# A causal mask cut into one operation per pair of heads, in a fused attention and mixture-of-experts kernel

## The chip, the cores and the metric

The kernel runs on one core of a Trainium2 chip. The metric is device time in microseconds (us) of one execution. Engines are called PE (TensorE, matrix multiplication), DVE (VectorE), ACT (ScalarE), POOL (GpSimd) and SP (SyncE, which only issues transfers here).

## What is computed

One transformer layer on x of shape (8, 1024, 256): eight batches, 16 heads of 16 columns. Biases and the second half's expert selection are left out of this cut:

```
h = layernorm(x)
Q, K, V = h @ Wq + bq, h @ Wk + bk, h @ Wv + bv            # 16 heads of 16
logits = where(causal, Q K^T * 0.25, -inf)                  # (8, 16, 1024, 1024)
attn   = softmax(logits)
gate   = a small network of h, one number per key
x = x + ((attn * gate) @ V) @ Wo + bo
x = x + shared_expert(layernorm(x)) + two_of_eight_experts(layernorm(x))
```

The causal mask sets a probability to zero where the key comes later than the query.

## The kernel before

**Tiling.** Batch n is worked in four groups g of four heads, and each group in ten steps s. A step takes a chunk c of 512 queries and one or two tiles of 128 keys. `STEPS` lists them: for the first chunk key tile 0, then tiles 1 and 3 together, then tile 2; for the second chunk tiles 0, 1, 2, 3 and 4 one by one, then 5 and 7 together, then 6. In all but the two steps of tile 2 and tile 6 `by_pair` is true and the step's scores are made in `PAIRS` = 2 parts p, each for two heads. So a group has 8 steps of two parts and 2 steps of one part (`SCORES`). Keys of a step's tile lie along the partitions and queries along the columns.

**A step.** The item names are those of the planner, and the functions in brackets make the instructions:
- `QK` (`scores`) on PE multiplies keys by queries, once for each part p.
- `EX` (`exponent`) on ACT takes the exponential of two heads, 128x1024, into `probs`. That tile has two halves, and step s uses half s % 2. In a one-part step `EX` does all four heads at once.
- `MK` (`mask`) on POOL zeroes the triangle of a diagonal tile, 128 keys by 128 queries, in each head. Only six of a group's ten steps touch the diagonal (`DIAGONAL`): tile 0; 1 and 3; 2; 4; 5 and 7; 6. Steps with two tiles have two triangles.
- `PV` (`sums`) on PE multiplies the probabilities by the gated values. It waits for the mask where there is one, and for the last exponential where there is none. `PV` of step s frees the half of `probs` that step s + 2 writes.

**What runs beside it.** For later batches: row maxima of the scores (`M` on PE, `MR` on DVE), projections (`AQ`, `AV`) and the gate network, whose products with `ln_g`, `ln_b` and `dp_w2`, and `gt`, are POOL's. For earlier batches: the output projection, the router, the experts (`EU`, `HT`, `ED`), the scatter of tokens into slots of their experts (`SX`, line 1157, a DMA that POOL issues) and the gather and mix of results (`GY`, `CB`, `CC`, POOL too).

**The order.** Nothing but the queue's own order and semaphores decides what an engine does next. The order is made ahead by a planner, `Plan.run`: each item has an engine, a duration in its tables and a due time, and the planner takes, on the engine that can start first, the ready item that is due earliest. It also hands out the eight PSUM banks, and it prefers on PE an item of the same tiling (`FULL`, `ROWS` for `M` and `QK`, `COLS` for `PV`). Where the planner expects PE to be idle for 500 ns or more while sums are open, `keep_busy` (line 809) puts filler matmuls of 128x512 there. A changed duration or a changed list of items therefore changes the whole order behind the first place where it matters.

Of the kernel before, what the change touches and what calls it, by code (L numbers as in the profile page):

```python
# [13 lines left out]
P = 128  # L14
# [4 lines left out]
GROUP = 4  # L19
# [40 lines left out]
SCORES = [PAIRS if by_pair else 1 for _, _, by_pair in STEPS]  # L60
NSCORE = sum(SCORES)
DIAGONAL = [kts[0] >= c * QPC for c, kts, _ in STEPS]
MASKS = sum(DIAGONAL)

MAXU = [(c,) + u for c in range(CHUNKS) for u in maxima_of(c)]
NMAX = len(MAXU)
# [95 lines left out]
def step_parts(s):  # L162

    c, kts, _ = STEPS[s]
    parts, at = [], 0
    for kt in kts:
        q0 = max(c * CHUNK, kt * P)
        parts.append((kt, q0, (c + 1) * CHUNK - q0, at))
        at += (c + 1) * CHUNK - q0
    return parts  # L170
# [22 lines left out]
class Plan:  # L193
# [9 lines left out]
    def add(self, engine, item, ns, due, after=(), banks=0, tiling=None, frees=None, lands=None, spaced=None, early=0):  # L203
        self.items[item] = (engine, ns, due + LATER.get(item[0], 0), [a for a in after if a in self.items], banks, tiling, frees, lands)
        self.early[item] = early
        if spaced and spaced[0] in self.items:
            self.spaced[item] = spaced
        self.queues.setdefault(engine, {}).setdefault(item[0], []).append(item)
# [77 lines left out]
def plan_work():  # L286
    plan = Plan()
    add = plan.add

    def sums(cols, rate=0.96):  # L290
        return round(cols / rate)
# [3 lines left out]
    def step_due(n, g, s):  # L295
        return at(n, g) + GROUP_T * step_at[s] // step_at[NSTEP]
# [93 lines left out]
    def attention(n, g, s):  # L390
        c, kts, by_pair = STEPS[s]
        gs = (n * GROUPS + g) * NSTEP + s
        cols = sum(part[2] for part in step_parts(s))
        due = step_due(n, g, s)
        before = [("PV",) + divmod((gs - 2) // NSTEP, GROUPS) + ((gs - 2) % NSTEP,)] if gs > 1 else []
        for p in range(SCORES[s]):
            add("PE", ("QK", n, g, s, p), 270 + 60 * (SCORES[s] == 1 or len(kts) > 1), due + p * 1200,
                [("SM", n, g, c)] + before, 2, ROWS)
            add("ACT", ("EX", n, g, s, p), 170 + sums(2 * CHUNK, 1.2), due + p * 1200, [("QK", n, g, s, p)],
                frees=(("QK", n, g, s, p), None))  # L400
        ready = [("EX", n, g, s, p) for p in range(SCORES[s])]
        if DIAGONAL[s]:
            add("POOL", ("MK", n, g, s), 650 * len(kts), due + 1500, ready)
            ready.append(("MK", n, g, s))
        add("PE", ("PV", n, g, s), 100 * len(kts) + round(cols * 4 / 2.4), due + 4000, ready + [("VA", n, g)],
            int(s in FIRST_STEP), COLS)
        if s in LAST_STEP:
            first = ("PV", n, g, FIRST_STEP[c])
            u = (n * GROUPS + g) * CHUNKS + c
            add("ACT", ("OE", n, g, c), 490, due + 4000, [("PV", n, g, s)] + (  # L410
                [("SO", (u - 1) // (GROUPS * CHUNKS), (u - 1) // CHUNKS % GROUPS, (u - 1) % CHUNKS)] if u else []),
                frees=(first, None))
            add("SP", ("SO", n, g, c), ISSUE, due + 4000, [("OE", n, g, c)], lands=6000)
# [148 lines left out]
    for n in range(B):  # L562
        projection(n)
        gate(n)
        if n == 0:
            for i in range(FFN_CHUNKS):
                weights(i)
        for g in range(GROUPS):
            values(n, g)
            maxima(n, g)  # L570
            if g + n * GROUPS:
                pn, pg = divmod(n * GROUPS + g - 1, GROUPS)
                for s in range(NSTEP):
                    attention(pn, pg, s)
        if n:
            rest(n - 1)
    for s in range(NSTEP):
        attention(B - 1, GROUPS - 1, s)
# [4 lines left out]
def build(nc, ins, out):  # L583
    x_in = ins["x"]
    plan = plan_work()
    order, place, waits, release = plan.order, plan.place, plan.waits, plan.release
    turn_of = {item: k for k, item in enumerate(order["PE"])}
    with ExitStack() as ctx:
        def sb(name, shape, dt=F32):
            return ctx.enter_context(nc.sbuf_tensor(name, shape, dt))  # L590

        def sem(name):
            return ctx.enter_context(nc.semaphore(name))
# [68 lines left out]
        probs = sb("probs", [P, 2, GROUP, CHUNK])  # L662
# [63 lines left out]
        s_full, p_masked, pv_done = sem("s_full"), sem("p_masked"), sem("pv_done")  # L726
# [15 lines left out]
        def bank(item, j=0):  # L742
            return ps[:, place[item][j], :]
# [73 lines left out]
        block = ctx.enter_context(nc.Block())  # L817
# [194 lines left out]
        def _(pool):  # L1012
            heard = {}

            def first_wait(name, count):
# [13 lines left out]
                                    pattern=[[-1, P]], channel_multiplier=1).then_inc(const_set, 1)  # L1029
            nc.gpsimd.affine_select(out=causal, in_=causal, compare_op=ALU.is_ge, fill=NEG, base=0,  # L1030
                                    pattern=[[1, P]], channel_multiplier=-1).then_inc(const_set, 1)
            nc.gpsimd.affine_select(out=before8[:], in_=before8[:], compare_op=ALU.is_gt, fill=0.0, base=0,
                                    pattern=[[1, EXPERTS], [-1, EXPERTS]], channel_multiplier=0
                                    ).then_inc(const_set, 1)
            nc.gpsimd.affine_select(out=earlier[:], in_=earlier[:], compare_op=ALU.is_gt, fill=0.0, base=0,
                                    pattern=[[1, P]], channel_multiplier=-1).then_inc(const_set, 1)
# [80 lines left out]
                        gate[:].unsqueeze(2).to_broadcast([P, TILES, DH]), ALU.mult)  # L1117
                last.then_inc(va_built, 1)

            def mask(item, n, g, s):  # L1120
                b, k = release["EX", n, g, s, SCORES[s] - 1]
                pool.wait_ge(freed[b], k)
                for _, _, _, at in step_parts(s):
                    block = probs[:, s % 2, :, at:at + P]
                    last = nc.gpsimd.affine_select(out=block, in_=block, compare_op=ALU.is_ge, fill=0.0, base=0,  # L1125
                                                   pattern=[[0, GROUP], [1, P]], channel_multiplier=-1)
                last.then_inc(p_masked, 1)

            def normalise(item, n, q):
# [54 lines left out]
            def split_ffn(item, i):  # L1184
                if i == 0:
# [5 lines left out]

            all_work(pool, "POOL", {"PK": constants, "AR": rstd_a, "GB": gate_rstd, "GD": gate_scale, "GF": gate_dot1,
                                    "GH": gate_hidden, "GJ": gate_dot2, "VA": build_values, "MK": mask,
                                    "CP": normalise, "CK": rstd_c, "SX": scatter_tile, "GY": gather_tile,
                                    "CB": mix_one, "CC": mix_two,
# [598 lines left out]
        def _(pe):  # L1794
# [5 lines left out]
            def wait_freed(b, k):  # L1800

                if passed[b] < k:
                    pe.wait_ge(freed[b], k)
                    passed[b] = k

            def own_banks(item):
                for b, k in waits[item]:
                    wait_freed(b, k)
# [83 lines left out]
            def sums(item, n, g, s):  # L1892
                gi = n * GROUPS + g
                c = STEPS[s][0]
                first = ("PV", n, g, FIRST_STEP[c])
                if s == 0:
                    pe.wait_ge(va_built, gi + 1)
                if s in FIRST_STEP:
                    own_banks(item)
                if DIAGONAL[s]:  # L1900
                    pe.wait_ge(p_masked, gi * MASKS + sum(DIAGONAL[:s + 1]))
                else:
                    b, k = release["EX", n, g, s, SCORES[s] - 1]
                    wait_freed(b, k)
                for kt, q0, cols, at in step_parts(s):
                    for h in range(GROUP):
                        last = mm(bank(first)[32 * h:32 * h + 32, q0 - c * CHUNK:], vaug[:, kt, g, h * VW:h * VW + 32],  # L1907
                                  probs[:, s % 2, h, at:at + cols], start=(s in FIRST_STEP), stop=(s in LAST_STEP))
                last.then_inc(pv_done, 1)
# [120 lines left out]
            def expert_down(item, n, q, u):  # L2030
# [9 lines left out]
                for i in range(2):  # L2040
# [6 lines left out]
                    for j, (h, w) in enumerate(((h_hi, w2_hi), (h_hi, w2_lo), (h_lo, w2_hi))):  # L2047
# [4 lines left out]

            all_work(pe, "PE", {"AT": turn_x, "AV": values, "AQ": queries_keys, "M": maximum, "MT": turn_max,
                                "QK": scores, "PV": sums, "CW": project, "CT": turn_x2, "CG": logits, "CJ": turn_logits, "PX": place,
                                "XT": turn_slots, "EU": expert_up, "HT": turn_h, "ED": expert_down})

# [34 lines left out]
```

## Time and profile before

| | |
|---|---|
| median of 3 runs | 1828.57 us |
| lowest and highest | 1823.91 and 1830.67 us |
| span of the profiled execution | 1826.8 us, 1.8 under the median |
| other time given for the profiled execution | none, so its span stands for it |
| busy PE, DVE, ACT, POOL | 1667.4, 1297.7, 1084.0, 767.8 us |
| PE idle | 1826.8 - 1667.4 = 159.4 us |

An engine's busy time is the union of its instructions' times. PE's weight loads (PEld) lie beside its matmuls. Matmuls overlap each other's ends, so a busy PE isn't one at its peak. "Idle before" is the time an engine stood still before an instruction, and the name behind the arrow is what ended that.

### The profile page before, as it was taken

How to read it: one execution, taken by the hardware profiler on the slowest of the kernel's cores; microseconds unless marked ns; L12 is line 12 of the kernel's file. 1: busy time of each engine (PE TensorE's matmuls, PEld its weight loads, DVE VectorE, ACT ScalarE, POOL GpSimd, SP SyncE). 2: the span in 40 equal slices, each digit the busy share in tenths (PEclk: the TensorE clock that was granted, in tenths of full speed). 3: DMA queues.
4: the chain of work that ended last, by engine and by line, in shares of the span. 5: the costliest groups of instructions: out<-in, count | busy, mean ns of one | idle time of the engine just before them, and what ended most of it. 6: DMA issues, size and time to landing. Idle time of an engine off the chain costs nothing.

```text
span 1826.8 us, 34347 instructions
## 1 busy us (share of the span) xinstructions
PE 1667.4 (91%) x12734; PEld 997.3 (55%) x12734; DVE 1297.7 (71%) x2528; ACT 1084.0 (59%) x1808; POOL 767.8 (42%) x1126
## 2 busy tenths in 40 slices
PE   7798899989987999899998899999998989998798
PEld 4343356435643566456554555555664656666677
DVE  4867777967796678777686666778678657873556
ACT  2565755665556656575557756576556756568432
POOL 4424432452236211632227862353116773057760
PEclk9698999989998999999998999989999899999899
DMA  4566545554345544544434765544435674346430
GB/s 152 160 192 182 164 153 157 164 149 125 99 122 137 142 121 119 158 118 141 140 113 143 213 180 143 146 125 122 132 102 152 199 204 142 94 138 203 141 121 13
DMA packets 192707, 261.24 MB, mean 143 GB/s; under 512 B 19616, under 2 KB 127264, under 8 KB 192544
## 3 DMA queue, kind: packets, MB, share of 16 engines
q1 hardware_dynamic: 181792, 229.67, 42.9%
q0 software_dynamic: 10752, 29.37, 5.5%
q8 instruction: 105, 1.72, 0.4%
q14 instruction: 58, 0.48, 0.1%
HBM read 130.98 MB, written 127.40 MB: 141 GB/s over the span
## 4 chain that ended last, share of the span: by engine, by line
PE 44%; DMA 16%; DVE 13%; POOL 8%; ACT 7%; SPq 5%; issue 5%; DVEq 0%; POOLq 0%; ACTq 0%
PE ps_all L2017 9%; PE ps_all L1907 7%; DVE mx L1496 6%; DMA qk_s<-ql 5%; PE ps_all L2048 5%; PE ps_all L1855 5%; ACT probs L1307 4%; PE ps_all L1887 4%; PE ps_all L1839 3%; DMA xa<-in_x 3%; PE ps_all L1916 2%; PE ps_all L1825 2%; SPq L889 2%; DMA yab<-ys_s,slot_u 2%; POOL xs_s L1157 2%
## 5 line engine op out<-in xcount | busy, mean ns | idle before, releaser
L1496 DVE TENSOR_REDUCE mx<-ps_all 128x2 f32<-128x1024 f32 (+2 forms) x640 | 616.9, 1005 | 131.1 <-PE ps_all L1862 71.2
L1307 ACT ACTIVATE probs<-ps_all 128x1024 f32<-128x1024 f32 x576 | 569.2, 1027 | 185.6 <-PE ps_all L1887 182.4
L1125 POOL TENSOR_SCALAR_AFFINE_SELECT probs<-probs 128x512 f32<-128x512 f32 x256 | 160.2, 641 | 569.4 <-ACT probs L1307 567.9
L1907 PE MATMUL ps_all<-probs,vaug 128*32 128x512 f32 (+3 forms) x3072 | 323.6, 521 | 25.2 <-POOL probs L1125 22.0
L1855 PE MATMUL ps_all<-k_st,q_st 63*128 63x512 f32 (+3 forms) x1536 | 306.3, 432 | 32.5 <-DVE mx L1496 12.1
L1887 PE MATMUL ps_all<-q_st,k_st 64*128 64x512 f32 (+3 forms) x1536 | 264.2, 404 | 45.0 <-DVE mx L1496 18.5
L1855 PEld LDWEIGHTS ps_all<-k_st,q_st 63*128 63x128 f32 x1536 | 155.1, 198 | 155.4 <-issue 52.4
L1887 PEld LDWEIGHTS ps_all<-q_st,k_st 64*128 64x128 f32 x1536 | 131.3, 193 | 173.9 <-issue 67.5
L1751 DVE SCALAR_TENSOR_TENSOR act_t<-act_t,ps_all 128x256 f32<-128x256 f32 x168 | 70.4, 419 | 151.8 <-ACT act_t L1370 150.9
L2017 PE MATMUL ps_all<-w_hi,x2h 128*128 128x512 f32 (+1 forms) x480 | 167.7, 349 | 2.5 <-DVE ql L1458 1.2
L2017 PE MATMUL ps_all<-w_hi,x2l 128*128 128x512 f32 (+1 forms) x480 | 157.8, 329 | 0.0
L2017 PE MATMUL ps_all<-w_lo,x2h 128*128 128x512 f32 (+1 forms) x480 | 157.7, 329 | 0.0
L1370 ACT ACTIVATE act_t<-ps_all 128x256 f32<-128x256 f32 x168 | 64.4, 384 | 153.5 <-PE ps_all L2017 106.1
L1907 PEld LDWEIGHTS ps_all<-probs,vaug 128*32 128x32 f32 x3072 | 72.7, 111 | 140.5 <-issue 88.5
L1157 POOL DMA_INDIRECT xs_s<-xnb,slot_u x112 | 110.8, 989 | 69.8 <-issue 50.8
L1862 PE MATMUL ps_all<-bars 64*128 64x64 bf16 x2048 | 123.8, 201 | 0.0
L1169 POOL DMA_INDIRECT yab<-ys_s,slot_u x112 | 108.1, 965 | 34.0 <-issue 19.2
L2048 PE MATMUL ps_all<-w_hi,h_hi 128*128 128x256 f32 (+1 forms) x336 | 109.8, 327 | 2.0 <-DVE h_lo L1778 1.1
L2017 PEld LDWEIGHTS ps_all<-w_hi,x2h 128*128 128x128 f32 x480 | 92.2, 192 | 20.6 <-issue 11.6
L1825 PE MATMUL ps_all<-wvd,xt 128*128 128x384 f32 x256 | 98.7, 514 | 1.5 <-DMA vd_bias<-in_dp_b 0.7
L2017 PEld LDWEIGHTS ps_all<-w_hi,x2l 128*128 128x128 f32 x480 | 91.8, 191 | 8.3
L2017 PEld LDWEIGHTS ps_all<-w_lo,x2h 128*128 128x128 f32 x480 | 92.3, 192 | 5.9
(195 smaller groups left out, 2810.1 us busy)
## 6 DMA issues: line engine op xcount, KB each, us to landing
qk_s<-qh SPq DMA_DIRECT2D x116, 256.0 KB
q_st<-qk_s SPq DMA_DIRECT2D x128, 192.0 KB, 3.9
k_st<-qk_s SPq DMA_DIRECT2D x128, 192.0 KB, 4.7
xs<-xs_s SPq DMA_DIRECT2D x72, 256.0 KB
ys_s<-ysb SPq DMA_DIRECT2D x72, 256.0 KB, 3.5
o_s<-o_sb SPq DMA_DIRECT2D x64, 256.0 KB, 4.4
qk_s<-ql SPq DMA_DIRECT2D x57, 256.0 KB
xs_s<-ysb SPq DMA_DIRECT2D x20, 512.0 KB, 5.5
```

The source lines that it names most:

```text
L1125: last = nc.gpsimd.affine_select(out=block, in_=block, compare_op=ALU.is_ge, fill=0.0, base=0, pattern=[[0, GROUP], [1, P]], channel_multi ...
L1157: nc.gpsimd.indirect_dma_start(xs_s[i % 2], bass.IndirectOffsetOnAxis(ap=slot_u[:, n % 4, a, t:t + 1], axis=0), xnb[:, t, :], None).then_i ...
L1169: nc.gpsimd.indirect_dma_start(yab[:, t % 2, a, :], None, ys_s[SET_OF[n] % 2], bass.IndirectOffsetOnAxis(ap=slot_u[:, n % 4, a, t:t + 1], ...
L1307: nc.scalar.activation(to, of, ACT.Exp, scale=DH ** -0.5).then_inc(freed[release[item][0]], 1)
L1496: last = nc.vector.tensor_reduce(to[:, :, p, qt % QPC], both[:, :, at:at + keys], X_AXIS, ALU.max)
L1825: last = mm(bank(item)[:, 0:E + DP], xt[:, k, tt * P:(tt + 1) * P], wvd[:, k, :], start=(k == 0), stop=(k == KE - 1))
L1855: last = mm(bank(item, j)[:, to:to + keys], q_st[r, q_half(n, g, c), p, qt % QPC * P:(qt % QPC + 1) * P], k_st[r, k_half(n, g, kc), p, 0:k ...
L1862: last = mm(bank(item, j)[:, end:end + P // 2], bars[r, h, 1, :], bars[r, h, 0, lo:lo + P // 2], start=False, stop=(h == 1))
L1887: last = mm(bank(item, j)[:, to:to + cols], k_st[r, k_half(n, g, kt // QPC), a, kt % QPC * P:(kt % QPC + 1) * P], q_st[r, q_half(n, g, c), ...
L1907: last = mm(bank(first)[32 * h:32 * h + 32, q0 - c * CHUNK:], vaug[:, kt, g, h * VW:h * VW + 32], probs[:, s % 2, h, at:at + cols], start= ...
L2017: last = mm(bank(item)[:, to], x[:, buf, k, t * P:(t + 1) * P], w[:, k, cs], start=(k == 0 and j == 0), stop=(k == KE - 1 and j == 2))
L2048: last = mm(bank(first)[:, t * E:(t + 1) * E], h[:, z % 2, i * P:(i + 1) * P], w[:, cs], start=(item == first and i == 0 and j == 0), stop ...
```

## The change

The mask of a two-part step becomes two items, one for each part p: `MK` p waits only for `EX` p, and covers the two heads of that part. The mask of a one-part step stays one item over four heads. A group's 6 mask items become 2 x 5 = 10. Of affine selects a group had 8, each over 4 heads x 128 columns (512); it now has 12 over 2 x 128 (256) and 2 over 512. Over 32 groups that is 256 before, and 384 small and 64 of the old size now. In the planner's tables a mask item goes from 650 ns for each tile to 380 ns for each tile in a two-part step, and its due time from 1500 behind the step's to 300 for part 0 and 1500 for part 1. `PV` waits for both masks.

```
-MASKS = sum(DIAGONAL)
+MASKS = sum(n for n, d in zip(SCORES, DIAGONAL) if d)
...
         ready = [("EX", n, g, s, p) for p in range(SCORES[s])]
         if DIAGONAL[s]:
-            add("POOL", ("MK", n, g, s), 650 * len(kts), due + 1500, ready)
-            ready.append(("MK", n, g, s))
+            for p in range(SCORES[s]):
+                add("POOL", ("MK", n, g, s, p), 650 if SCORES[s] == 1 else 380 * len(kts), due + p * 1200 + 300, [ready[p]])
+            ready += [("MK", n, g, s, p) for p in range(SCORES[s])]
...
-            def mask(item, n, g, s):
-                b, k = release["EX", n, g, s, SCORES[s] - 1]
+            def mask(item, n, g, s, p):
+                b, k = release["EX", n, g, s, p]
                 pool.wait_ge(freed[b], k)
+                heads = GROUP // SCORES[s]
                 for _, _, _, at in step_parts(s):
-                    block = probs[:, s % 2, :, at:at + P]
+                    block = probs[:, s % 2, p * heads:(p + 1) * heads, at:at + P]
                     last = nc.gpsimd.affine_select(out=block, in_=block, compare_op=ALU.is_ge, fill=0.0, base=0,
-                                                   pattern=[[0, GROUP], [1, P]], channel_multiplier=-1)
+                                                   pattern=[[0, heads], [1, P]], channel_multiplier=-1)
                 last.then_inc(p_masked, 1)
...
-                    pe.wait_ge(p_masked, gi * MASKS + sum(DIAGONAL[:s + 1]))
+                    pe.wait_ge(p_masked, gi * MASKS + sum(SCORES[i] for i in range(s + 1) if DIAGONAL[i]))
```

The new order differs nearly everywhere. Counted in the two orders: PE changes its tiling 914 times before and 940 after, there are 84 filler matmuls before and 100 after, and 21 of 192 mask items stood right behind a scatter before, 25 of 320 now.

POOL's queue during the scatters of batch 1, with batch 2's group 2 in attention. Before, the rows at L1125 are the masks of (n, g, s) = (2, 2, 7), then the two triangles of (2, 2, 8), then (2, 2, 9); L1157 is the scatter and L1093 to L1103 the gate network of batch 3:

```order
L1125 AFFINE_SELECT probs<-probs 128x4x128
L1157 DMA xs_s<-xnb,slot_u 5120x256
L1093 TENSOR_TENSOR gt<-drift,small 128x128
L1097 TENSOR_TENSOR gt<-gt,small 128x128
L1157 DMA xs_s<-xnb,slot_u 5120x256
L1125 AFFINE_SELECT probs<-probs 128x4x128 x2
L1157 DMA xs_s<-xnb,slot_u 5120x256
L1103 TENSOR_TENSOR gt<-gt,small 128x128
L1157 DMA xs_s<-xnb,slot_u 5120x256
L1125 AFFINE_SELECT probs<-probs 128x4x128
```

The same place now, where the masks' line is L1127 and the scatter's L1159:

```order
L1159 DMA xs_s<-xnb,slot_u 5120x256
L1127 AFFINE_SELECT probs<-probs 128x2x128
L1060 TENSOR_TENSOR mv_a<-mv_a,minus_one 128x2
L1061 TENSOR_TENSOR rs_a<-ve_a,minus_half 128x2
L1063 TENSOR_TENSOR mv_a<-mv_a,rs_a 128x2
L1159 DMA xs_s<-xnb,slot_u 5120x256
L1104 TENSOR_TENSOR gt<-gt,small 128x128
L1159 DMA xs_s<-xnb,slot_u 5120x256
L1127 AFFINE_SELECT probs<-probs 128x2x128 x3
L1159 DMA xs_s<-xnb,slot_u 5120x256
L1127 AFFINE_SELECT probs<-probs 128x2x128 x2
```

The first select is part 0 of step 7. Part 1 of step 7 stands with part 0 of step 8 in the "x3". So two scatters stand now between the two parts of step 7, and one between those of step 8. In the whole order 95 of the 128 pairs of mask items are neighbours and 33 have other work between them, 9 scatters among it.

PE's queue at the first place where it differs, batch 0, group 1, steps 7 to 9. Before (L1887 is `QK`, L1825 `AV`, L1907 `PV`, L1855 and L1862 `M`, L1839 `AQ`):

```order
L1887 MATMUL ps_all<-q_st,k_st 128x128 x2
L1825 MATMUL ps_all<-wvd,xt 128x384 x2
L1907 MATMUL ps_all<-probs,vaug 32x512 x4
L1855 MATMUL ps_all<-k_st,q_st 128x256 x2
L1862 MATMUL ps_all<-bars 128x64 x4
L1855 MATMUL ps_all<-k_st,q_st 128x256 x2
L1862 MATMUL ps_all<-bars 128x64 x4
L1887 MATMUL ps_all<-q_st,k_st 128x256 x4
```

And now, with the lines moved by two:

```order
L1889 MATMUL ps_all<-q_st,k_st 128x128 x2
L1909 MATMUL ps_all<-probs,vaug 32x512 x4
L1827 MATMUL ps_all<-wvd,xt 128x384 x2
L1841 MATMUL ps_all<-xt,wk 128x512 x2
L1857 MATMUL ps_all<-k_st,q_st 128x256 x2
L1864 MATMUL ps_all<-bars 128x64 x4
L1857 MATMUL ps_all<-k_st,q_st 128x256 x2
L1864 MATMUL ps_all<-bars 128x64 x4
L1889 MATMUL ps_all<-q_st,k_st 128x256 x4
```

`PV` of step 7, whose mask the planner now expects earlier, moved ahead of the projection that stood before it. Over all steps, 2140 PE items stood between the last `QK` of a step and its `PV` before, and 2067 do now.

## Rows read from the trace of the kernel before

**Rows 1.** The page's first lines: span, busy time of each engine.
```profile
span 1826.8 us, 34347 instructions
PE 1667.4 (91%) x12734; PEld 997.3 (55%) x12734; DVE 1297.7 (71%) x2528; ACT 1084.0 (59%) x1808; POOL 767.8 (42%) x1126
```

**Rows 2.** The page's chain that ended last, shares of the span by engine.
```profile
PE 44%; DMA 16%; DVE 13%; POOL 8%; ACT 7%; SPq 5%; issue 5%; DVEq 0%; POOLq 0%; ACTq 0%
```

**Rows 3.** The page's costliest groups: busy us, mean ns | idle before, releaser.
```profile
L1307 ACT ACTIVATE probs<-ps_all 128x1024 f32<-128x1024 f32 x576 | 569.2, 1027 | 185.6 <-PE ps_all L1887 182.4
L1125 POOL TENSOR_SCALAR_AFFINE_SELECT probs<-probs 128x512 f32<-128x512 f32 x256 | 160.2, 641 | 569.4 <-ACT probs L1307 567.9
```

**Rows 4.** The chain of waits: us in total, times, longest us.
```profile
POOL probs L1125 <- ACT probs L1307: 567.9, 105, 26.5
...
POOL xs_s L1157 <- issue: 50.8, 102, 5.6
...
PE ps_all L1907 <- POOL probs L1125: 22.0, 23, 5.5
```

**Rows 5.** PE's groups with shapes kept apart: PV by its first tile's columns.
```profile
L1907 PE MATMUL ps_all<-probs,vaug 128*32 128x512 f32 x1536 | 219.4, 651 | 8.2 <-POOL probs L1125 5.6 <-issue 1.2 <-DVE mx L1496 0.6
...
L1907 PE MATMUL ps_all<-probs,vaug 128*32 128x384 f32 x512 | 55.7, 507 | 3.6 <-POOL probs L1125 3.2
...
L1907 PE MATMUL ps_all<-probs,vaug 128*32 128x256 f32 x512 | 41.3, 395 | 13.4 <-POOL probs L1125 13.2
```

**Rows 6.** Timeline of ACT, POOL and PE, 622 to 632 us: start, us, engine.
```profile
622.83 3.78 ACT L1307 ACTIVATE probs<-ps_all 128x1024 f32<-128x1024 f32 x4
624.85 0.64 POOL L1125 TENSOR_SCALAR_AFFINE_SELECT probs<-probs 128x512 f32<-128x512 f32 x1 [1.96 <-ACT probs L1307]
626.68 1.23 POOL L1125 TENSOR_SCALAR_AFFINE_SELECT probs<-probs 128x512 f32<-128x512 f32 x2 [1.19 <-ACT probs L1307]
630.79 1.07 PE L1907 MATMUL ps_all<-probs,vaug 128*32 128x384 f32 x16
```

**Rows 7.** POOL's groups by shape: the select over 128 columns.
```profile
L1028 POOL TENSOR_SCALAR_AFFINE_SELECT ident<-ident 128x128 f32<-128x128 f32 x1 | 0.3, 287 | 0.2 <-POOL before L1026 0.2
```

**Rows 8.** Timeline of PE, 704 to 705 us: same tiling, then PV's.
```profile
704.01 0.60 PE L1980 MATMUL ps_all<-ident,xs 128*128 128x128 f32 x4
704.45 0.60 PE L1924 MATMUL ps_all<-ident,xnb 128*128 128x128 f32 x4
704.98 0.64 PE L1907 MATMUL ps_all<-probs,vaug 128*32 128x512 f32 x4
```

**Rows 9.** PE's filler matmuls: their group, and four rows of the timeline.
```profile
L809 PE MATMUL ps_all<-bars,scan 128*64 128x512 bf16 x84 | 29.4, 426 | 0.0
...
174.94 1.92 PE L809 MATMUL ps_all<-bars,scan 128*64 128x512 bf16 x4
176.78 0.79 PE L1855 MATMUL ps_all<-k_st,q_st 63*128 63x512 f32 x2
...
184.54 1.48 PE L809 MATMUL ps_all<-bars,scan 128*64 128x512 bf16 x6
188.38 0.69 PE L1855 MATMUL ps_all<-k_st,q_st 63*128 63x384 f32 x2 [2.36 <-DVE mx L1496]
```

**Rows 10.** Timeline of POOL, 568 to 577 us: a mask queued behind a scatter.
```profile
568.63 0.46 POOL L1103 TENSOR_TENSOR gt<-gt,small 128x128 f32<-128x128 f32 x1
574.71 1.02 POOL L1157 DMA_INDIRECT xs_s<-xnb,slot_u  x1 [5.62 <-issue]
575.74 0.65 POOL L1125 TENSOR_SCALAR_AFFINE_SELECT probs<-probs 128x512 f32<-128x512 f32 x1
```

**Rows 11.** Timeline of PE: its three longest waits for a mask.
```profile
388.57 0.64 PE L1907 MATMUL ps_all<-probs,vaug 128*32 128x256 f32 x8 [3.73 <-POOL probs L1125]
...
576.44 1.08 PE L1907 MATMUL ps_all<-probs,vaug 128*32 128x256 f32 x8 [5.53 <-POOL probs L1125]
...
1412.64 1.06 PE L1907 MATMUL ps_all<-probs,vaug 128*32 128x512 f32 x8 [3.16 <-POOL probs L1125]
```

## The prediction

> **What bounds the kernel now.** I read the page's busy times first. PE is busy for 1667.4 us of 1826.8, which leaves 159.4 us, and POOL, the engine that the change loads, for 767.8, which leaves 1059 [rows 1]. The chain that ended last says the same: PE has 44% of it and POOL 8% [rows 2]. Then I looked for what the change could shorten. The costliest groups show 256 selects of 641 ns, and in front of them 569.4 us in which POOL stood still, nearly all of it for the exponential [rows 3]. So the mask usually waits for its data. Whether anybody waits for the mask is what counts, and the chain of waits answers: PE stood still for it 23 times, 22.0 us in all, the longest 5.5 [rows 4]. That is 1.2% of the span and a bound on everything that shorter masks alone can give.
>
> PE's groups by shape split these 22.0 us, since the first tile of a step has 512, 384 or 256 columns. A `PV` that begins with 512 columns waited 5.6 us for masks, one with 384 waited 3.2, and one with 256 waited 13.2 [rows 5]. The last are the steps of tile 2 and tile 6, which have one part; their masks aren't changed. What is left for the change is 5.6 + 3.2 = 8.8 us.
>
> A typical step shows why it is so little. Four exponentials follow each other in 3.78 us; the mask of the first step begins at 624.85, the two triangles of the second end at 626.68 + 1.23 = 627.91, and the `PV` that reads them starts at 630.79, 2.9 us later [rows 6]. PE had other work and wasn't waiting.
>
> **The change part by part.**
>
> *Cost of the small select.* No row before has a select over 256 columns. The neighbours are 641 ns at 512 columns [rows 3] and 287 at 128 [rows 7]. A straight line gives 287 + (641 - 287) x 128 / 384 = 405 ns. The bounds are 287, if columns were free up to there, and 641, if the number of columns didn't matter. I take 405, since 256 lies between two measured sizes, nearer to the smaller.
>
> *What it takes off the latency.* Part 0's mask runs while ACT makes part 1's exponential, which lasts 1027 ns [rows 3]: 405 fits into it, and so do the two selects of a two-tile step, 810. Behind the last exponential there remain 405 in place of 641, or 810 in place of 1282 (two rows of 641; the pair of rows 6 took 1230). The saving is 0.24 or 0.42 to 0.47 us for a step, 0.35 as a middle. The average wait for a mask is 22.0 / 23 = 0.96 us [rows 4], so 8.8 us are about nine waits, and nine times 0.35 is 3.2 us. The bounds are 0 (the planner gives `PV` an earlier place by as much, so PE arrives earlier and waits as before) and 8.8. I take **-3.2**.
>
> *What it adds on POOL.* 384 x 0.405 + 64 x 0.641 - 256 x 0.641 = 155.5 + 41.0 - 164.1 = +32.4 us of busy time, and between -12.8 (287 ns) and +123 (641 ns). The 1059 us in which POOL stands still cover all of these, 568 us of them right before a mask [rows 4]. I cost it at 0. If the cover is gone, because other items of POOL queue up behind a mask that waits for its exponential, the ones behind are the products of the gate network, the scatters and the small operations of the layer norms. 95 of the 128 pairs of masks are neighbours in the new queue and change nothing there, so this touches the other 33 at most.
>
> *The new order on PE: tiling.* There are 26 more changes of tiling, 940 for 914. In the timeline the transposes at 704.01 end at 704.61 and the next ones of the same tiling start at 704.45, an overlap of 0.16; these end at 705.05 and `PV`, in another tiling, starts at 704.98, an overlap of 0.07 [rows 8]. A change costs 0.09 us, and 26 cost **+2.3**. The bounds are 0, where PE had to wait there anyway, and 4.7 at twice this. The Trainium skill has a rule that speaks against this part of the change: TensorEngine Tiling (Array Packing), Key Properties, says that changing the tiling mode drains the engine. The trace agrees with its direction; the page gives no price, and without the rows one would have to charge each of the 26 with the time of a whole matmul.
>
> *Filler matmuls.* 16 more, 100 for 84. One takes 29.4 / 84 = 0.35 us [rows 9]. They are free where PE waits anyway and cost their length where it doesn't, and the trace has both: behind the six of 184.54 PE still stood 2.36 us, behind the four of 174.94 it went straight on [rows 9]. I take half: 16 x 0.35 / 2 = **+2.8**, with 0 and 5.6 as bounds.
>
> *The rest of the new order* moves nearly all items by a few places and changes no item's work. It makes new accidents in the 159 us that PE stands still, and takes old ones away. I see no sign for its sum. I give it 0, and 6% of the 159, some 10 us, as what it may do to either side: about as much as the three longest waits of rows 11 together.
>
> The sum, against the profiled execution's span: 1826.8 - 3.2 + 2.3 + 2.8 = 1828.7. The median of the runs lies 1.8 above that span, so the forecast is **1830**.
>
> **The rivals.** A measurement of this kernel tells about 0.5% from no change, 9 us; that is faster below 1819 and slower above 1838.
>
> *A (0.43): the masks are off PE's path.* As worked out, 1830, its own range 1820 to 1838. For it speak the 2.9 us between mask and `PV` and the 1.2% bound.
>
> *B (0.24): faster.* The 8.8 us go wholly, since `PV` of the changed steps never comes too early, and of the waits in unchanged steps the two longest, 5.53 and 3.73 us [rows 11], were accidents of the old order and go with it. 1828.6 - 8.8 - 9.3 + 5.1 = 1816. For it speaks that halves of `probs` come free sooner, and that 73 fewer PE items (2067 for 2140) stand between the scores and their `PV`. Against it, PE has 91% busy time, and a step freed sooner adds nothing to an engine that has work.
>
> *C (0.29): slower, masks behind scatters.* POOL's queue is strictly in order. At 568.63 it did a small product, ended it at 569.09, then stood 5.62 us at a scatter, and the mask behind came at 575.74 [rows 10]; PE waited 5.53 us for it [rows 11]. The scatters' own stops come to 50.8 us in 102 places [rows 4]. Two more of PE's waits have the same form, 3.73 and 3.16 us, a mean of 4.1 for the three [rows 11]. Now 25 masks stand right behind a scatter for 21, and nine scatters stand between the two parts of a step, which they could not before. `PV` needs both parts, so a scatter that stops there holds PE. With four more of them PE loses 4 x 4.1 = 16.4 us, giving 1830 + 16 = 1846. It decides from two or three on, where it passes 1838. Against it, the average stop of a scatter is 50.8 / 102 = 0.5 us, and only the long ones reach PE.
>
> *D (0.04): the small select isn't cheaper.* At 641 ns for 256 columns nothing is saved behind the last exponential, POOL carries 123 us more, and the time is 1830 + 3.2 = 1833. The 287 ns at 128 columns speak against it [rows 7].
>
> **How the numbers follow.** The predicted time is A's, 1830. B is faster and C is slower, except where they stay small: of each about a tenth falls within 0.5%, and a few of A's cases fall outside. That gives 0.25 faster, 0.44 the same and 0.31 slower. For 8 in 10 the range goes from 1811, a little below B's 1816, to 1848, a little above C's 1846; A's spread of 10 us around 1830 lies inside it.
>
> **What would show it.** In the profile of the changed kernel: 448 selects, the small ones near 0.40 us, POOL's busy time near 800 us. PE's wait for masks from 22.0 to something between 13 and 30; below 13, with a shorter span, B is right, above 30 C is, and then the long ones must have a scatter ahead of the mask. PE busy within 10 us of 1667. The prediction is wrong if PE's idle time moves by more than 10 us to either side while its waits for masks move by less than 5: then the new order did it, by waits that I priced at nothing.

## The result

| | before | changed |
|---|---|---|
| median of 20 runs | 1829.15 us | 1819.1 us |
| lowest and highest | 1820.32, 1835.84 | 1811.46, 1825.31 |
| ratio, with its 95% interval | | 0.9946 [0.9931, 0.9961] |
| span of the profiled execution | 1826.8 us | 1815.1 us |

The changed kernel is 0.5% faster. The time lies in the range of the prediction, and the forecast, no change, is wrong. It was timed again in two later series (runs e5 and e16 below): 0.9959 [0.9939, 0.9978] and 0.9988 [0.9964, 1.0012]. Weighted by their intervals the three give 0.9958, so 0.4% is the better figure. It isn't firm: the first and the last of the three intervals don't overlap, and in the two later series the kernel before stood at 1846 us, not at 1829.

The page of the changed kernel: span, busy times, the granted clock in 40 slices.

```profile
span 1815.1 us, 34564 instructions
...
PE 1650.4 (91%) x12750; PEld 985.3 (54%) x12750; DVE 1298.6 (72%) x2528; ACT 1080.0 (60%) x1808; POOL 797.3 (44%) x1318
...
PEclk9699999999998999999999989999999999999999
```

Against [rows 1] PE's busy time fell by 17.0 us, and its idle time rose, from 159.4 to 1815.1 - 1650.4 = 164.7. The same matmuls and 16 fillers more took less time. So the gain isn't in anything that PE waits for. It is in the speed at which PE worked, and the granted clock points to it. This is the clock's row of before:

```profile
PEclk9698999989998999999998999989999899999899
```

The view of the cores gives the mean granted clock of either profiled execution, 0.951 before and 0.966 after:

```profile
core 0: 1826.8 us, clock 0.951
```

```profile
core 0: 1815.1 us, clock 0.966
```

The 0.966 is the highest clock of the changed kernel's 20 runs; their mean is 0.961. For the kernel before the later series give means of 0.951 to 0.953.

Next POOL's groups by shape and PE's sums of the changed kernel, to set beside [rows 3, 5, 7]:

```profile
L1127 POOL TENSOR_SCALAR_AFFINE_SELECT probs<-probs 128x256 f32<-128x256 f32 x384 | 150.5, 412 | 443.4 <-ACT probs L1309 441.3
...
L1127 POOL TENSOR_SCALAR_AFFINE_SELECT probs<-probs 128x512 f32<-128x512 f32 x64 | 41.1, 642 | 89.2 <-ACT probs L1309 89.0
```

```profile
L1909 PE MATMUL ps_all<-probs,vaug 128*32 128x512 f32 x1536 | 215.8, 639 | 9.8 <-POOL probs L1127 4.7 <-issue 2.1 <-DVE ql L1460 1.3
...
L1909 PE MATMUL ps_all<-probs,vaug 128*32 128x384 f32 x512 | 55.3, 503 | 6.8 <-POOL probs L1127 6.6
L1909 PE MATMUL ps_all<-probs,vaug 128*32 128x256 f32 x512 | 41.4, 395 | 12.4 <-POOL probs L1127 11.9
```

And the chain of waits, the rows that answer to [rows 4]:

```profile
POOL probs L1127 <- ACT probs L1309: 530.3, 179, 33.5
...
POOL xs_s L1159 <- issue: 40.3, 103, 5.1
...
PE ps_all L1909 <- POOL probs L1127: 23.2, 26, 4.3
```

A small select takes 412 ns where 405 was estimated, and POOL's busy time rose by 29.5 us where 32.4 was. PE waits 23.2 us for masks, not less than the 22.0 of before. In the changed steps the waits went from 8.8 to 4.7 + 6.6 = 11.3 us.

**What the clock does.** One stop of PE, at the scatter of [rows 10] and the wait of [rows 11]. The view is that of windows of the kernel before; its columns are the window, its length, PE's busy time, the granted clock, and DMA:

```profile
560.00:570.90 10.90, 10.69 (x105) 1.00 0.48 124
570.90:576.40 5.50, 0.01 (x2) 0.77 0.54 140
576.40:584.10 7.70, 7.66 (x55) 0.50 0.37 138
584.10:594.10 10.00, 8.15 (x58) 1.00 0.66 156
```

PE worked at the full clock of 2.4 GHz, stood still for 5.5 us, the clock fell to 0.50 (1.2 GHz) during the stop, and stayed there for 7.7 us of work. By this trace a long stop costs its own length and up to half of the 7.7 us behind it, an estimate from the two levels. The changed kernel has stops of this kind too, one at the mask of (1, 2, 9):

```profile
380.80:385.10 4.30, 0.01 (x1) 0.89 0.51 138
385.10:391.00 5.90, 5.90 (x48) 0.50 0.35 124
391.00:401.00 10.00, 9.51 (x73) 1.00 0.48 117
```

At 576 us it has none. Other work of POOL and PE stands there, and the longest stop of a scatter among that work is 0.98 us:

```profile
565.36 0.98 POOL L1159 DMA_INDIRECT xs_s<-xnb,slot_u  x1 [0.98 <-issue]
566.35 0.78 POOL L1127 TENSOR_SCALAR_AFFINE_SELECT probs<-probs 128x256 f32<-128x256 f32 x2
```

Four microseconds later it has another one, of 3.07 us, in which PE waits for a transfer and not for a mask. The clock falls there too, as the windows from 576 and from 586 us show:

```profile
583.53 0.69 PE L1982 MATMUL ps_all<-ident,xs 128*128 128x128 f32 x2 [3.07 <-DMA xs<-xs_s]
```

```profile
576.00:586.00 10.00, 5.54 (x45) 0.81 0.75 206
586.00:596.00 10.00, 9.69 (x55) 0.85 0.36 108
```

As the clock has two levels, the time at the low one is 2 x (1 - mean) x span: about 179 us before, and 2 x 0.034 x 1815.1 = 123 us after. The stretches at the low level, added up in the two traces, are 177.7 us in 27 pieces and 123.6 us in 19, and PE was busy for 158.1 and 102.0 us of them. What the low level costs is seen in two rows with the same eight matmuls of `PV`, 1.07 us at granted clock 1.00 in the changed kernel and 1.94 us at 0.50 in e9 (shown again below):

```profile
563.72 1.07 PE L1909 MATMUL ps_all<-probs,vaug 128*32 128x512 f32 x8
```

At that factor of 1.8, 56 us of busy time fewer at the low level save 56.1 x (1 - 1 / 1.8) = 25 us, an estimate. PE's busy time fell by 17.0. So the new order also takes some 8 us more of PE's time than the old one at one and the same clock, 1.6 of them for the fillers; no run splits the rest.

Stops of PE over 1.5 us, a bound that I chose for counting, number 26 before, 73.6 us in all, and 19 after, 61.7 us. So PE stands still as long in sum, but in fewer long pieces, and has 54 us less of low clock. The runs agree in size: over the 380 runs of the later series, each taken against the mean of its own kernel and series, 0.01 more of granted clock goes with 10.2 us less (correlation -0.63). For the 0.008 to 0.010 between the mean clocks that is 8 to 10 us. The measured difference of the two medians is 10. No run changed the clock alone, so the clock as the way by which the order gains rests on these counts and on the correlation.

### The profile page after: what moved, and what is told of

Read it like the earlier page. It is cut to its first block, busy times and chain, and to the rows that moved or that the text cites. A ratio compares the mean times of both kernels' runs of the same rounds, so it can differ in the third digit from the quotient of the medians.

```text
span 1815.1 us, 34564 instructions
## 1 busy us (share of the span) xinstructions
PE 1650.4 (91%) x12750; PEld 985.3 (54%) x12750; DVE 1298.6 (72%) x2528; ACT 1080.0 (60%) x1808; POOL 797.3 (44%) x1318
## 4 chain that ended last, share of the span: by engine, by line
PE 47%; DVE 15%; DMA 12%; POOL 11%; ACT 6%; issue 5%; SPq 4%; POOLq 0%; DVEq 0%; ACTq 0%
PE ps_all L2019 10%; DVE mx L1498 8%; PE ps_all L1909 8%; PE ps_all L1857 5%; PE ps_all L1889 5%; PE ps_all L2050 4%; PE ps_all L1841 3%; ACT probs L1309 3%; PE ps_all L1827 3%; POOL xs_s L1159 3%; DMA yab<-ys_s,slot_u 3%; DMA qk_s<-ql 2%; PE ps_all L1918 2%; POOL yab L1171 2%; POOL probs L1127 2%
## 5 line engine op out<-in xcount | busy, mean ns | idle before, releaser
L1127 POOL TENSOR_SCALAR_AFFINE_SELECT probs<-probs 128x256 f32<-128x256 f32 (+1 forms) x448 | 191.2, 445 | 532.6 <-ACT probs L1309 530.3
L1909 PE MATMUL ps_all<-probs,vaug 128*32 128x512 f32 (+3 forms) x3072 | 318.8, 515 | 28.9 <-POOL probs L1127 23.2
L1857 PE MATMUL ps_all<-k_st,q_st 63*128 63x512 f32 (+3 forms) x1536 | 300.2, 426 | 47.7 <-DVE mx L1498 20.8
L1857 PEld LDWEIGHTS ps_all<-k_st,q_st 63*128 63x128 f32 x1536 | 151.4, 195 | 169.3 <-DVE mx L1498 53.0
L1159 POOL DMA_INDIRECT xs_s<-xnb,slot_u x112 | 110.4, 985 | 58.7 <-issue 40.3
```

Source lines behind the costliest of these rows:

```text
L1159: nc.gpsimd.indirect_dma_start(xs_s[i % 2], bass.IndirectOffsetOnAxis(ap=slot_u[:, n % 4, a, t:t + 1], axis=0), xnb[:, t, :], None).then_i ...
L1857: last = mm(bank(item, j)[:, to:to + keys], q_st[r, q_half(n, g, c), p, qt % QPC * P:(qt % QPC + 1) * P], k_st[r, k_half(n, g, kc), p, 0:k ...
```

## The experiments

The theories at the start. **L**: the shorter, earlier masks make the gain. **O**: the new order makes it, through fewer long stops and a higher clock. **C**: within O, the 16 fillers more hold the clock up. Ratios are to the kernel before on the same chip, with the 95% interval; the clocks are means over all runs of this kernel and of the kernel before in its series. A series is a set of kernels timed on one chip at one time: e1 to e4, e5 to e8, e9 to e11, e12 to e15, e16 to e18.

| run | ratio | interval | clock, this / before |
|---|---|---|---|
| e1, split masks, old order | 1.0021 | 0.9995 to 1.0047 | 0.949 / 0.953 |
| e18, the same again | 0.9992 | 0.9975 to 1.0009 | 0.950 / 0.951 |
| e2, whole masks, new order | 0.9985 | 0.9962 to 1.0009 | 0.959 / 0.953 |
| e17, the same again | 0.9971 | 0.9954 to 0.9987 | 0.958 / 0.951 |
| e5, changed kernel again | 0.9959 | 0.9939 to 0.9978 | 0.957 / 0.951 |
| e16, the same a third time | 0.9988 | 0.9964 to 1.0012 | 0.955 / 0.951 |
| e3, before without fillers | 0.9980 | 0.9957 to 1.0004 | 0.946 / 0.953 |
| e4, changed without fillers | 0.9956 | 0.9930 to 0.9982 | 0.949 / 0.953 |
| e11, before with 176 fillers | 0.9987 | 0.9966 to 1.0008 | 0.957 / 0.953 |
| e6, table 380, whole masks | 1.0041 | 1.0019 to 1.0063 | 0.956 / 0.951 |
| e7, table 660, whole masks | 1.0022 | 0.9994 to 1.0050 | 0.952 / 0.951 |
| e8, table 640, whole masks | 0.9977 | 0.9953 to 1.0000 | 0.954 / 0.951 |
| e9, before, three masks moved | 0.9976 | 0.9952 to 1.0001 | 0.956 / 0.953 |
| e10, changed, masks ahead of scatters | 0.9960 | 0.9935 to 0.9985 | 0.960 / 0.953 |
| e12, table 400, split | 0.9995 | 0.9969 to 1.0020 | 0.956 / 0.953 |
| e13, the same order, whole | 1.0006 | 0.9981 to 1.0031 | 0.958 / 0.953 |
| e14, table 325, split | 1.0041 | 1.0018 to 1.0064 | 0.955 / 0.953 |
| e15, the same order, whole | 1.0056 | 1.0032 to 1.0081 | 0.954 / 0.953 |

**Split or order: e1 and e2, e16 to e18.** e1 splits the masks and leaves the planner's list alone:

```
             def mask(item, n, g, s):
-                b, k = release["EX", n, g, s, SCORES[s] - 1]
-                pool.wait_ge(freed[b], k)
-                for _, _, _, at in step_parts(s):
...
+                heads = GROUP // SCORES[s]
+                for p in range(SCORES[s]):
+                    b, k = release["EX", n, g, s, p]
+                    pool.wait_ge(freed[b], k)
+                    for _, _, _, at in step_parts(s):
+                        block = probs[:, s % 2, p * heads:(p + 1) * heads, at:at + P]
```

> The masks are cut into pairs of heads, each behind its own exponential, but every queue keeps the order of the kernel before. Theory L (shorter, earlier masks make the gain): ratio to before 0.994 to 0.996, PE's wait for masks falls from 22 to under 15 us. Theory O (the new order makes it, the masks themselves nothing): ratio 0.998 to 1.002, at most 3 us faster.

e2 takes the changed kernel's order, makes nothing at the first item of a pair, and the whole mask at the second:

```
             def mask(item, n, g, s, p):
+                if p < SCORES[s] - 1:
+                    return
                 b, k = release["EX", n, g, s, p]
...
+                    block = probs[:, s % 2, :, at:at + P]
```

> The order of the changed kernel on every queue, but a mask is one operation over four heads behind both exponentials, as before. L: ratio 0.999 to 1.003, since the masks are as late as before and the order counts on earlier ones. O: ratio 0.994 to 0.996, granted clock about 0.96, and PE's wait for masks 2 to 8 us above the 23 of the changed kernel.

The split alone does nothing that these timings can tell: 1.0021 and, in e18, 0.9992. PE's wait for masks was 19.4 us in e1 and 17.5 in e18, against 22.0 before:

```profile
PE ps_all L1909 <- POOL probs L1127: 19.4, 20, 5.4
```

```profile
PE ps_all L1909 <- POOL probs L1127: 17.5, 18, 4.7
```

That isn't clear of the spread between single profiles either. e11 has whole masks and the old order, with more fillers, and waits as little; and e17, with whole masks in the new order, waits no longer than the changed kernel's 23.2:

```profile
PE ps_all L1907 <- POOL probs L1125: 19.2, 18, 4.2
```

```profile
PE ps_all L1910 <- POOL probs L1128: 21.8, 32, 4.2
```

The order alone gives 0.9985 and 0.9971, weighted 0.9976 with an interval of 0.9962 to 0.9989, and this with whole masks. e2 by itself decided nothing, since 0.9985 lies between what L and O had expected and its interval reaches 1; e17 is clear of 1. L falls. O stands, with about half of the gain: the order alone was never timed beside the changed kernel where that gained 0.5%. The last series put all corners on one chip:

> The changed kernel beside its two halves on one chip. Ratio 0.995, within 0.993 to 0.997. With a worth of the split of 0.1%, as under the two orders of e12 to e15, the order carries the rest: then e17 is at 0.996 to 0.997.

> The changed kernel's order with whole masks, the program of e2. If the order carries the gain: 0.996 to 0.997, within 0.2% of e16. If split and order gain only together: 0.998 to 1.000, 0.3% or more above e16.

> The old order with split masks, the program of e1. If the split is worth 0.1% under any order: 0.998 to 1.000. If it costs under an order that isn't made for it, as e1 hinted: 1.001 to 1.003.

There the whole masks in the new order (0.9971) were no slower than the split ones (0.9988), and their intervals overlap. The changed kernel itself missed its expectation of 0.993 to 0.997. The busy times of the three pages, e16, e17, e18, repeat the picture of the first pair: PE's busy time is 13 to 14 us lower with the new order, whichever masks it has. The profiled executions of e16 and e17 were 9 and 7 us faster than their medians, that of e18 1 us slower, so a part of this difference is chance:

```profile
span 1832.7 us, 34564 instructions
...
PE 1659.3 (91%) x12750; PEld 989.0 (54%) x12750; DVE 1295.8 (71%) x2528; ACT 1080.0 (59%) x1808; POOL 799.3 (44%) x1318
```

```profile
span 1830.9 us, 34372 instructions
...
PE 1660.7 (91%) x12750; PEld 986.9 (54%) x12750; DVE 1298.5 (71%) x2528; ACT 1080.8 (59%) x1808; POOL 766.2 (42%) x1126
```

```profile
span 1844.3 us, 34539 instructions
...
PE 1673.6 (91%) x12734; PEld 1001.6 (54%) x12734; DVE 1298.9 (70%) x2528; ACT 1081.5 (59%) x1808; POOL 797.0 (43%) x1318
```

In all six profiles with the new order and its fillers PE has 16 to 19 stops over 1.5 us (the changed kernel three times, e2, e17, e10) and 124 to 155 us of low clock; in all five with the old one it has 26 to 29 (before, e1, e18, e9, e11) and 178 to 195 us.

**Is it a draw: e5 to e8.**

> The changed kernel itself, beside its relatives on one chip: 0.9946 again, within 0.993 to 0.997, if the gain is a property of the program and not of the chip that it was first timed on. If orders answer to a chip's transfer times by accident, anything from 0.993 to 1.000.

e6 to e8 change one number of the planner's table, with whole masks: 650 becomes `650 if SCORES[s] == 1 else 380` in e6, 660 in e7, 640 in e8.

> The kernel before with one number of the planner's table changed: a mask of a two-part step counts 380 ns a tile in place of 650, while the operation stays whole. The order moves as far from the old one as the changed kernel's does (99 fillers, 930 changes of tiling, PE items moved by 2.8 places on average). O in the form 'an order that expects masks earlier is better': ratio 0.994 to 0.997. O in the form 'accidents of an order': anything between 0.994 and 1.006, unrelated to the masks.

> The kernel before with 660 ns a tile in the table in place of 650: a change of no meaning, which moves PE's items by 2.2 places on average. Accidents of an order: a ratio off 1 by 0.2% to 0.6%, to either side. If only meaningful changes of the order count: 0.999 to 1.001.

> The same with 640 ns in place of 650 (PE's items moved by 1.4 places, 76 fillers for 84). Accidents of an order: off 1 by 0.2% to 0.6%, and not by the same as with 660. Otherwise 0.999 to 1.001.

A change of 10 ns in a table that describes 641 ns moves the time by +0.2% and -0.2%, and the shorter number by +0.4%. The intervals of e7 and e8 just touch 1, but the two differ from each other by more than the noise. So this order, which expects masks earlier, isn't better for that, and one order differs from the next by as much as the change under study gained.

**More orders, split and whole: e12 to e15.** The edits are 400 or 325 for the change's 380 in its table, and those of e2 for the whole masks.

> The changed kernel with 400 ns a tile in the planner's table for a mask of a pair, in place of 380: another order of the same family (97 fillers, 933 changes of tiling, PE's items moved by 3.2 places against before), with split masks. If an order that knows of split masks gains with them (S): ratio 0.994 to 0.997. If the gain of the changed kernel is one lucky order (A): anywhere in 0.996 to 1.004, like the three orders of e6 to e8.

> The order of e12 on all queues with whole masks over four heads behind both exponentials. S: 0.2% to 0.5% slower than e12. A: within 0.2% of e12.

> The changed kernel with 325 ns a tile in the table (85 fillers, 929 changes of tiling). S: ratio 0.994 to 0.997. A: anywhere in 0.996 to 1.004.

> The order of e14 with whole masks. S: 0.2% to 0.5% slower than e14. A: within 0.2% of e14.

Two more orders planned for split masks came out at 0.9995 and 1.0041. Split masks change the time by -0.11% and -0.15% under them, less than an interval; with e16 against e17 (+0.17%) and e1 and e18 against before (+0.21%, -0.08%) the five pairs average to 0.0%, and none of them is resolved. The changed kernel's order is a favourable draw among the six new orders that were timed; with whole masks e8's 0.9977 is as good as its 0.9976. Its granted clock is no cause that stands alone either: e6, e13 and e14 have a clock 0.002 to 0.006 above before and are slower or level. At the slope of 10.2 us for 0.01, e6 and e14 lose about 11 us in other ways. Their profiles say that much of it is waiting. Against e12, on the same chip, e14 has the same busy time of PE (1668.2 and 1667.3 us), but 176.8 us of idle time for 169.1, and PE's wait for masks is 28.9 us for 17.0. Against e5, e6 has 10.4 us more idle time and 7.3 us more busy time. Long stops don't settle the clock either: e14 has 27 of them, as many as an old order, and 155 us of low clock, as few as e2. Each of these is a single execution.

**Fillers: e3, e4, e11.** e3 and e4 make the condition of `keep_busy` false; e11 changes its constants:

```
-IDLE_FROM, IDLE_KEPT, IDLE_STEP = 500, 300, 230
+IDLE_FROM, IDLE_KEPT, IDLE_STEP = 400, 0, 230
```

> The kernel before without its 84 filler matmuls. If fillers keep the clock up (theory C, the 16 more of them make the gain): slower, ratio 1.005 to 1.015, granted clock under 0.945. If they only cost (as the prediction had it): ratio 0.993 to 0.999.

> The changed kernel without its 100 filler matmuls. C: it loses its lead, and lands within 0.2% of the kernel before without fillers. O without C: it stays 0.4% to 0.6% below that kernel.

> The kernel before with more filler matmuls in the same order, 176 for 84 (they begin at 400 ns of expected idle time, and fill it all). If fillers buy clock for more than they cost: ratio 0.994 to 0.998, clock up by 0.005 or more. From the kernels without fillers, where 84 fewer lowered the clock by 0.007 and left the time within 0.2%: 0.998 to 1.004.

Without fillers the clock falls, by 0.007 in e3 and in e4 by some 0.01 below the changed kernel of other series, and the time doesn't rise. With twice as many it rises by 0.0035, and the time is within 0.2%. They buy as much as they cost. The changed kernel without any filler is at 0.9956, clear of 1, so its lead over the kernel before doesn't hang on fillers. C falls. Its lead over e3, 0.9956 to 0.9980, is hardly more than the noise.

**Scatters: e9 and e10.** e9 moves three masks in POOL's queue, e10 exchanges each mask right behind a scatter with it:

```
+    queue = order["POOL"]
+    for mask, by in ((("MK", 1, 2, 9), 1), (("MK", 2, 2, 9), 1), (("MK", 6, 2, 7), 2)):
+        i = queue.index(mask)
+        queue.insert(i - by, queue.pop(i))
```

> The kernel before, with three mask items moved in POOL's queue: those of (n, g, s) = (1, 2, 9) and (2, 2, 9) ahead of the scatter in front of them, that of (6, 2, 7) ahead of a scatter and a product of the gate network. In the trace of before PE stood 3.7, 5.5 and 3.2 us for these three, and the low clock that followed lasted 6.8, 10.2 and 10.2 us. If a long stop costs its length alone: up to 12 us less, minus what PE then waits for instead, ratio 0.995 to 0.999, clock unchanged. If it also costs the clock behind it: ratio 0.990 to 0.995, granted clock up by 0.003 to 0.008. If POOL's stop only moves to the next waiter: 0.998 to 1.001.

> The changed kernel, with each mask that stood right behind a scatter put ahead of it (30 exchanges). If stops behind scatters still cost it: ratio 0.990 to 0.994 to before. If the few that reach PE are no more than others: 0.994 to 0.997, as without the exchange.

e9 shows what moving them does at one of the three places. POOL's timeline, and PE's at the same place:

```profile
564.42 0.64 POOL L1129 TENSOR_SCALAR_AFFINE_SELECT probs<-probs 128x512 f32<-128x512 f32 x1 [0.29 <-ACT probs L1311]
569.27 1.02 POOL L1161 DMA_INDIRECT xs_s<-xnb,slot_u  x1 [4.21 <-issue]
570.60 0.96 POOL L1161 DMA_INDIRECT xs_s<-xnb,slot_u  x1 [0.30 <-issue]
571.59 1.47 POOL L1119 TENSOR_TENSOR vaug<-vh,gate 128x128 f32<-128x128 f32 x4
573.22 1.01 POOL L1161 DMA_INDIRECT xs_s<-xnb,slot_u  x1 [0.17 <-issue]
574.25 0.65 POOL L1129 TENSOR_SCALAR_AFFINE_SELECT probs<-probs 128x512 f32<-128x512 f32 x1
```

```profile
575.05 1.94 PE L1911 MATMUL ps_all<-probs,vaug 128*32 128x512 f32 x8 [5.56 <-POOL probs L1129]
```

The moved mask ran at once, at 564.42. The scatter still stopped for 4.21 us, and now the mask of the next step stood behind it and three other items, and PE waited 5.56 us there for the 5.53 of before. The stop went to the next waiter. Its 0.9976 isn't clear of 1, and its interval holds both a stop that costs its length alone and one that only moves. It lies above the 0.990 to 0.995 expected if the low clock behind the stops went as well; it didn't go, for behind the moved stop the clock stood at 0.50 again, for 6.8 us in place of 10.2. e10's 0.9960 is that of the changed kernel in other series; in its own that kernel wasn't timed. No version tried is clearly faster than the changed kernel.

## Why the prediction was wrong

**The step that failed** is "the rest of the new order", which the prediction gave 0 with the words "I see no sign for its sum". The runs showed about -0.24% for the order alone, some 4 us; of the 10 us on the first chip the order's part wasn't measured. That is more than any single term that was worked out. Its channel was missing from the sum altogether: the prediction priced a stop of PE at its length, and left out the low clock behind it, though the page's row of the clock and its 0.951 were there to read. The prediction's own sign of being wrong was a change of more than 10 us in PE's idle time. That moved by 5.3 us only, while PE's busy time, expected within 10 us of 1667, fell by 17.0. The bound for such accidents, 10 us to either side, was about right: the orders tried lie between 0.997 and 1.006 with whole masks. Most of them lie within 0.5% of 1, as do both repeats of the changed kernel, so no run shows that its 0.44 for no change was too high; the first series fell just outside. That 1819 lies in the range is owed to this allowance to either side, not to a mechanism that the prediction had named.

**-3.2 for the masks** isn't shown, neither as a wait nor as time. With the old order PE waits 19.4 and 17.5 us with split masks, and 22.0 and, in e11, 19.2 with whole ones. Under the other orders the pairs, split and whole, are 23.3 and 21.8 (e16, e17), 17.0 and 22.3 (e12, e13), 28.9 and 25.0 (e14, e15): to either side. With the old order the two ratios average to 1.000. This fits the bound of 0 that the prediction gave the term; the reason given there, that PE comes to `PV` earlier, wasn't tested.

**Cost of the small select and POOL's load:** 412 ns and +29.5 us, against 405 and +32.4. POOL covered it: e1 and e18 carry the same load, at no cost that their timings can tell.

**Fillers and tiling, +5.1.** 16 more fillers added 31.0 - 29.4 = 1.6 us of busy time (the row below against [rows 9]). They were a cost in the prediction; the runs without them show that cost and gain cancel. The 26 changes of tiling weren't tried by themselves. The Trainium skill's rule in TensorEngine Tiling (Array Packing), Key Properties, that a changed mode drains the engine, spoke for slower, and no run here tells its size. The prediction's price of 0.09 us comes from a single pair of rows with modelled ends, which still overlap by 0.07 us at the change [rows 8]. The estimate above, some 8 us more of PE's time at one clock, says that the new order does cost PE something, of the sign of this term.

```profile
L810 PE MATMUL ps_all<-bars,scan 128*64 128x512 bf16 x100 | 31.0, 396 | 0.0
```

**Rival B** named the right side and 1816, which is luck, for its reason was wrong: it let waits for masks vanish, and they grew by 1.2 us. One part of it held, that the two longest waits were accidents of the old order. The 5.53 went and the 3.73 became 4.3. **Rival C**, masks behind scatters, didn't come about as a loss. PE's longest wait for a mask, 4.3 us, does have a scatter ahead of it that stopped for 3.44 us, but such stops didn't grow in sum (40.3 us for 50.8), and e10, which exchanges 30 masks with the scatter ahead of them, changes nothing.

**What stays open:** why this order has fewer long stops than five others (22 to 27), how those came to 155 to 165 us of low clock in four of the five all the same, what makes PE wait longer in e6 and e14, and where the half of the changed kernel's gain lies that the order alone doesn't show. Each order moves hundreds of items, and no single exchange was found that carries it.

## What to carry to other kernels

When a planner makes the order, an edit of one operation is two changes, and the new order can outweigh the edit. Time the edit in the old order, the new order without the edit, and a few orders of the same kind that mean nothing (10 ns in a table), before a gain of half a per cent is put down to the operation. Where an engine is busy for nine tenths, look at busy time as well as at waits: if it moved with the same instructions, read the granted clock.

## What the hardware showed unexpectedly

Executions of one kernel differ by about 1% (the changed kernel's 20 runs from 1811 to 1825 us, the 35 of before in the series of e5 from 1837 to 1859), and their granted clock goes with a good part of it: in those 20 runs the correlation with the time is -0.78, at 10.5 us for 0.01. Series differ more than the change does, on at least four chips: the median of the kernel before was 1829 us in two series and 1840 to 1846 us in the four others.

The scatter issued by POOL can stand for 4 to 5.6 us before it starts, although its neighbours stand for 0.15 to 0.3 us. The DMA engines were busy for 0.54 of their time in the window at 571 us. A busy DMA isn't enough for it, though: between 566 and 576 us of the changed kernel their share is 0.78, and the three scatters that start there stood for 0.17 us each. The cause stays open. A mask moved out of its way leaves the stop there: 4.21 us in e9 for 5.62.
